# First edge layer of a two-layer graph network: one-hot and PSUM buffers four groups deep, sums added two groups later, gather indices loaded by SyncE

## What is computed

```python
h = maximum(layernorm(x), 0)                     # first layer: a graph convolution
deg = segment_sum(ones, dst); dinv = rsqrt(deg)
msg = (h @ W)[src] * (dinv[src] * dinv[dst])[:, None]
x = x + relu(segment_sum(msg, dst) + b)
h = maximum(layernorm(x), 0)                     # second layer: attention over the same edges,
att = exp(clip((q[src] . k[dst]) / 4, -10, 10))  # summed by src, 8 heads of 16
out = segment_sum(att / segment_sum(att, src)[src] * v[dst], src) + h
x = x + (out - mean) * rsqrt(var + 1e-6) * gamma + beta
```

## Time and profile before

| | us |
|---|---|
| median of three runs (2272.0 to 2273.41) | 2273.32 |
| span of the profiled execution (its own time is not given) | 2940.6 |
| busy: PE / DVE / ACT / POOL | 1840.2 / 1874.7 / 1279.6 / 1551.0 |
| gathers of the first edge layer, first to last issue | 120.0 to 1449.2 |
| gathers of the second, first to last issue | from about 1518 to 2860.1 |

### The profile page before, as it was taken

How to read it: one execution, slowest core, us unless ns; L and a number is a source line. 1 busy time by engine, 2 the same in 40 slices (tenths; PEclk the granted TensorE clock), 3 DMA queues, 4 the chain that set the end, 5 groups by cost and what they waited for, 6 DMA issues and landing times. The chain is left out here.

```text
span 2940.6 us, 44304 instructions
## 1 busy us (share of the span) xinstructions
PE 1840.2 (63%) x10257; PEld 1461.4 (50%) x10258; DVE 1874.7 (64%) x5089; ACT 1279.6 (44%) x3362; POOL 1551.0 (53%) x1594
## 2 busy tenths in 40 slices
PE   5323346767576676677776767676666676666662
PEld 4323334544344444344454656566556665656662
DVE  9858775655455755455775666666666666666666
ACT  8524345755465565556653323333223332322333
POOL 0256655665556565565434555545455555555544
PEclk7756667877778787878887888888888888888886
DMA  3211111111111111111116444445444544444453
GB/s 105 62 41 42 43 39 39 45 42 38 38 38 45 38 41 41 39 44 39 33 68 185 126 125 127 127 122 131 119 121 124 132 123 122 125 123 123 126 122 55
DMA packets 234145, 244.06 MB, mean 83 GB/s; under 512 B 32925, under 2 KB 195229, under 8 KB 233989
## 3 DMA queue, kind: packets, MB, share of 16 engines
q0 software_dynamic: 61136, 147.00, 18.5%
q1 hardware_dynamic: 142357, 81.55, 10.8%
q10 hardware_dynamic: 30624, 15.21, 2.2%
HBM read 225.01 MB, written 18.62 MB: 83 GB/s over the span
## 5 line engine op out<-in xcount | busy, mean ns | idle before, releaser
L303 POOL DMA_INDIRECT rows<-y_tab,idx x832 | 795.6, 956 | 589.8 <-issue 307.9
L1340 POOL DMA_INDIRECT x<-kv_tab,kv_idx x672 | 682.7, 1016 | 623.0 <-DVE msg L1392 403.9
L1563 PE MATMUL ps_kv<-kv_s,hot_low 128*128 x1362 | 406.0, 443 | 168.9 <-DVE hot_low L1364 90.0
L780 ACT ACTIVATE sort_v<-sort_t,staged,minus 128x128 f16<-128x128 f16 x914 | 360.7, 480 | 309.1 <-remote 243.1
L872 PE MATMUL ps_sort<-sort_hi,sort_v 128*128 128x496 f16 x1662 | 417.6, 403 | 117.3 <-issue 112.4
L619 DVE TENSOR_SCALAR sort_v<-iota_h,staged 128x128 f16<-128x128 f16 x748 | 243.2, 325 | 339.2 <-remote 269.0
L1550 PE MATMUL ps_m<-msg,x 128*128 128x136 f32 x1792 | 295.4, 315 | 243.4 <-DVE msg L1392 182.7
L830 PE MATMUL ps_sum<-rows,hot 128*128 128x128 f32 x1664 | 282.0, 323 | 250.3 <-issue 120.1
L1374 DVE TENSOR_TENSOR by_tile<-ps_q,x 128x512 f32<-128x512 f32 x224 | 154.5, 690 | 404.9 <-remote 257.4
L830 PEld LDWEIGHTS ps_sum<-rows,hot 128*128 128x128 f32 x1664 | 260.4, 235 | 271.8 <-issue 139.4
L1550 PEld LDWEIGHTS ps_m<-msg,x 128*128 128x128 f32 x1792 | 263.3, 219 | 263.1 <-issue 245.7
(11 more groups left out here) (290 smaller groups left out, 2072.2 us busy)
## 6 DMA issues: line engine op xcount, KB each, us to landing
weights<-tile_tab SPq DMA_DIRECT2D x114, 256.0 KB
x<-tile_tab SPq DMA_DIRECT2D x113, 256.0 KB
weights<-tile_tab ACTq DMA_DIRECT2D x58, 256.0 KB
rows<-y_tab,idx POOLq DMA_INDIRECT x832
x<-kv_tab,kv_idx POOLq DMA_INDIRECT x672
kv_tab<-kv_s SPq DMA_DIRECT2D x12, 512.0 KB
x<-x_in SPq DMA_DIRECT2D x1, 3328.0 KB, 13.3
out<-x SPq DMA_DIRECT2D x12, 256.0 KB
```

Source lines behind the costliest of these rows:

```text
L303: pool.indirect_dma_start(out=rows[:, k * SPAN + n, :], out_offset=None, in_=y_tab, in_offset=bass.IndirectOffsetOnAxis(ap=idx[:, k, n:n + ...
L780: last = nc.scalar.activation(to[:, k % 2, m, :], sort_t[:, k % 2, m, :], ACT.Relu, bias=staged[:, v, c:c + 1], scale=minus[:, v, c:c + 1])
L1340: pool.indirect_dma_start(out=rows[:, u, k, :], out_offset=None, in_=kv_tab, in_offset=bass.IndirectOffsetOnAxis(ap=idx[:, u, k:k + 1], ax ...
L1563: last = nc.tensor.matmul(ps_kv[:, k % 2, :], hot_low[:, w, k * P:(k + 1) * P], kv_s[:, ds(low + w, 1), :], start=w == 0, stop=w == WINDOW ...
```

## The change

- `idx` is filled by DMAs that SyncE issues straight from HBM (`load_idx`), 4 KB each, for the next body as soon as `rows_in[k]` says that this body's rows have landed. `src_c`, `set_idx` and `set_next` are gone, and with them one small ScalarE instruction per group.
- `hot` has four buffers and `more_hot` two. They lie in `h`, which has been stored to HBM by then; VectorE waits for that (`y_stored`) before its first one-hots.
- Each of the four groups has its own PSUM bank (`ps_group`), with the first and the second block's sums in its halves. VectorE adds the sums of group k-2 in step k, not those of k-1, and one-hots of group k wait for the sums of four groups earlier, not two. TensorE waits for `acc_done[k]` of four groups earlier.
- The sort keeps two banks in place of four: both parts use them. So `take_sorted(0, ...)` now stands at the border of the parts, behind the block of preparations, and TensorE waits for it (`part_taken`) before the second part.
- TensorE runs `move(k)` right behind the sums of group k, where it ran `move(k-1)` there.
- After the loops VectorE has two groups to add instead of one.

```diff
-            src_c = sb1("src_c", [P, ET + BODY], I32)
...
-            group_tab = sb1("group_tab", [1, BODIES + 1, 2, GROUPS + 2], I32)
-            more_tab = sb1("more_tab", [1, BODIES + 1, GROUPS + 1], I32)
+            group_tab = sb1("group_tab", [1, BODIES + 1, 2, GROUPS + 3], I32)
...
-            hot = sb1("hot0", [P, 2, SPAN, P])
-            more_hot = sb1("more_hot", [P, SPAN, P])
+            flat_h = h[:, :, :].rearrange("p j d -> p (j d)")
+            hot = flat_h[:, 0:GROUPS * SPAN * P].rearrange("p (k n d) -> p k n d", k=GROUPS, n=SPAN)
+            more_hot = flat_h[:, GROUPS * SPAN * P:(GROUPS + 2) * SPAN * P].rearrange("p (k n d) -> p k n d", k=2, n=SPAN)
...
-            ps_sum = [ps1(f"ps_sum{k}", [P, 512]) for k in range(2)]
+            ps_group = [ps1(f"ps_group{k}", [P, 2, 256]) for k in range(GROUPS)]
+            ps_sum, ps_more = ([bank[:, n, 0:D] for bank in ps_group] for n in range(2))
             ps_iota = ps1("ps_iota", [P, 512])
-            ps_more = ps1("ps_more", [P, 512])
...
-            ps_sort = [[ps1(f"ps_sort{n}{m}", [P, 512]) for m in range(2)] for n in range(2)]
-            ps_row, ps_cnt, ps_deg = ps_sort[0][0], ps_sort[0][1], ps_sort[1][0]
-            ps_run = ps_sort[1]
+            ps_sort = [ps1(f"ps_sort{m}", [P, 512]) for m in range(2)]
+            ps_deg = ps1("ps_deg", [P, 512])
+            ps_row, ps_cnt = ps_sort
+            ps_run = ps_sort
...
-                sp.dma_start(src_c[:, 0:ET], src_in).then_inc(in_rest, 16)
...
+                def load_idx(i, k):
+                    sp.dma_start(idx[:, k, :], src_in[:, ds(i * BODY + k * SPAN, SPAN)]).then_inc(idx_set[k], 16)
+                for k in range(GROUPS):
+                    load_idx(0, k)
...
                 sp.wait_ge(y_stored, 16 * (2 + Y_PARTS))
+                with sp.Fori(0, BODIES - 1) as i:
+                    for k in range(GROUPS):
+                        sp.wait_ge(rows_in[k], (i + 1) * (16 * SPAN))
+                        load_idx(i + 1, k)
...
                         pool.wait_ge(sum_done[k], i + 1)
-                        pool.wait_ge(idx_set[k], i + 1)
+                        pool.wait_ge(idx_set[k], (i + 1) * 16)
...
-                v.sem_inc(acc_done[GROUPS - 2], 1)
+                for k in range(2):
+                    v.sem_inc(acc_done[k], 1)
...
                     wait_positive(v, more_rel_set, more + b + 1)
-                    one_hots(more_hot[:, :, :], more_rel[:, :]).then_inc(more_ready, 1)
-                def add_more(b, more):
+                    one_hots(more_hot[:, k % 2, :, :], more_rel[:, :]).then_inc(more_ready, 1)
...
+                def wait_added_before(i, k):
+                    v.wait_ge(acc_done[(k + 1) % GROUPS], i + (2 if k == GROUPS - 1 else 1))
+                def add_last_block(i, k, lo, hi, more):
+                    with v.If(hi > lo):
+                        wait_added_before(i, k)
+                        v.wait_ge(sum_done[(k - 2) % GROUPS], i + (1 if k < 2 else 2))
+                        add_more(hi, (k - 2) % GROUPS, more)
+                def add_first_block(i, k, lo):
+                    wait_added_before(i, k)
+                    v.wait_ge(sum_done[(k - 2) % GROUPS], i + (1 if k < 2 else 2))
+                    add_first(lo, (k - 2) % GROUPS)
...
                     lows, highs, mores = tables(i)
                     for k in range(GROUPS):
-                        before, lo, hi = (k - 1) % GROUPS, lows[k + 1], highs[k + 1]
-                        with v.If(highs[k] > lows[k]):
-                            v.wait_ge(acc_done[(k - 2) % GROUPS], i + 1)
-                            add_more(highs[k], mores[k])
+                        lo, hi, more = lows[k + 2], highs[k + 2], mores[k + 2]
+                        add_last_block(i, k, lows[k], highs[k], mores[k])
                         with v.If(hi > lo):
-                            more = mores[k + 1]
                             with v.If(hi > lo + 1):
-                                v.wait_ge(acc_done[(k - 2) % GROUPS], i + 1)
-                                v.nop(nofuse=True)
                                 with v.Fori(lo + 1, hi) as b:
-                                    wait_positive(v, more_acc, more + b + 1)
                                     more_hots(i, k, b, more)
-                                    add_more(b, more)
-                            wait_positive(v, more_acc, more + hi + 1)
+                                    add_more(b, k, more)
                             more_hots(i, k, hi, more)
-                        v.wait_ge(sum_done[(k - 2) % GROUPS], i + (1 if k < 2 else 2))
+                        v.wait_ge(sum_done[k], i + 1)
                         v.wait_ge(rel_set, i * GROUPS + k + 1)
-                        one_hots(hot[:, k % 2, :, :], rel[:, k, :]).then_inc(hot_ready[k], 1)
+                        one_hots(hot[:, k, :, :], rel[:, k, :]).then_inc(hot_ready[k], 1)
                         beside(k, 0)
                         v.wait_ge(hot_ready[k], i + 2)
-                        v.wait_ge(acc_done[(k - 2) % GROUPS], i + 1)
-                        v.wait_ge(sum_done[before], i + (1 if k == 0 else 2))
-                        add_first(lows[k], before)
+                        add_first_block(i, k, lows[k])
                         if k < GROUPS - 1:
-                            relative(i, k + 1, lows[k + 2])
+                            relative(i, k + 1, lows[k + 3])
                         else:
-                            relative(i + 1, 0, lows[k + 2])
+                            relative(i + 1, 0, lows[k + 3])
                         beside(k, 1)
...
+                v.wait_ge(y_stored, 16 * (2 + Y_PARTS))
                 with v.Fori(0, RANK_BODIES) as i:
...
                     if part > 0:
-                        take_sorted(0, slice(0, WIDTH[0]), slice(0, WIDTH[0]))
                         sort_body(SORT_BODIES - 1, LAST_SORTS)
...
+                    take_sorted(0, slice(0, WIDTH[0]), slice(0, WIDTH[0]))
+                    v.sem_inc(part_taken, 1)
...
-                v.wait_ge(acc_done[GROUPS - 2], BODIES + 1)
-                v.nop(nofuse=True)
-                with v.If(highs[0] > lows[0]):
-                    add_more(highs[0], mores[0])
-                    wait_positive(v, more_acc, mores[0] + highs[0] + 2)
-                    v.nop(nofuse=True)
-                v.wait_ge(sum_done[GROUPS - 1], BODIES + 1)
-                add_first(lows[0], GROUPS - 1)
+                for k in range(2):
+                    add_last_block(BODIES, k, lows[k], highs[k], mores[k])
+                    add_first_block(BODIES, k, lows[k])
...
-                def set_idx(i, k):
-                    nc.scalar.activation(idx[:, k, :], src_c[:, ds(i * BODY + k * SPAN, SPAN)], ACT.Copy).then_inc(idx_set[k], 1)
-                def set_next(i, k):
-                    act.wait_ge(rows_in[k], (i + 1) * (16 * SPAN))
-                    set_idx(i + 1, k)
...
                         last.then_inc(v1_ready[k], 1)
-                        set_next(n + RANK_BODIES, k)
...
-                    if k < GROUPS - 1:
+                    if k < 2:
                         pe.sem_inc(sum_done[k], 1)
                     pe.sem_inc(moved[k], 1)
...
-                nc.tensor.matmul(ps_sum[1][:, 0:D], zeros_h[:, 0:P], zeros_h[:, 0:D], start=True, stop=True).then_inc(sum_done[GROUPS - 1], 1)
+                for k in range(2, GROUPS):
+                    nc.tensor.matmul(ps_sum[k], zeros_h[:, 0:P], zeros_h[:, 0:D], start=True, stop=True).then_inc(sum_done[k], 1)
...
-                        lo, hi, more = ends[k + 1], ends[GROUPS + 2 + k + 1], mores[k + 1]
+                        lo, hi, more = ends[k + 2], ends[GROUPS + 3 + k + 2], mores[k + 2]
                         early = last and k == GROUPS - 1
                         if early:
-                            beside(k - 1)
+                            beside(k)
                         pe.wait_ge(rows_in[k], (i + 1) * (16 * SPAN))
+                        pe.wait_ge(acc_done[k], i + 1)
                         with pe.If(hi > lo):
                             with pe.Fori(lo, hi) as b:
                                 wait_positive(pe, more_ready, more + b + 2)
                                 pe.nop(nofuse=True)
-                                sums(ps_more, k, more_hot, more_done)
+                                sums(ps_more[k], k, more_hot[:, k % 2], more_done)
                         pe.wait_ge(hot_ready[k], i + 2)
-                        pe.wait_ge(acc_done[(k - 2) % GROUPS], i + 1)
-                        sums(ps_sum[k % 2], k, hot[:, k % 2], sum_done[k])
-                        if k > 0 and not early:
-                            beside(k - 1)
-                    beside(GROUPS - 1)
+                        sums(ps_sum[k], k, hot[:, k], sum_done[k])
+                        if not early:
+                            beside(k)
...
+                    if part == 0:
```

(5 more changed lines are left out.)

53 lines of the change are left out of this document (24 added, 29 removed).

## The result

The changed kernel takes 2280.06 us (median of 12 runs, 2277.06 to 2283.27), the kernel before, run beside it, 2272.11 us (12 runs, 2270.45 to 2275.94). The ratio is 1.0031, 95% interval 1.0023 to 1.0040: **slower, by 8 us**. The forecast was 2264 us and faster; the time lies inside the range, on the other side.

What follows compares the result with a forecast made beforehand. POOL's gathers were taken to bound the sort bodies and VectorE, narrowly, the ranking ones. Terms -4.1 (index copy), -5.7 (later sums) and +0.5 (banks, border) gave -9.3 us: 2273.3 to 2264 us, range 2244 to 2283.

Steps and rivals of the forecast that it cites:

- The pitch: POOL's gathers start 1.25 us apart when nothing holds them, 0.95 busy and 0.30 issue, in the timed runs too.
- The floor: POOL's gathers and indirect DMAs plus stretches before, between and after the layers: 2158.4 us, 114.9 below the timed runs.
- the 667 us of the trace: Profiled execution 2940.6 us against 2273.3 timed; the gap was laid mostly to TensorE "issue" gaps peculiar to the profiled execution.
- The 15%: Share of the profiled execution's loss that the timed runs keep, 114.9 / 782.2 us; used to scale POOL's waits.
- the coupling's -5.7 us: Sums added two groups later with four buffers: TensorE and VectorE lose less to each other; bounds 0 and -25.7 us.
- Index copy at group 24, -4.1 us: Without ScalarE's index copy the gather of group 24 starts at 419.05, not 423.13 us, and the gain stays.
- Banks, border, start, tail, +0.5 us: Shared sort banks read out at the border, one more matmul, layer start, second add after the loops: between 0 and 2.
- Third rival, 2281 us: TensorE waits for ScalarE's sort tiles before the next sums, 2.5 us in each of 21 bodies; slower, chance 0.18.
- First rival, 2271 us: Gathers hide everything; only the lead at group 24 is won, or less; 2269 to 2273 us, no difference, chance 0.29.
- The span near 2900: The profiled execution's span should fall by about 40 us to 2900: the index copy's gain plus 22% of 174.9, 38.

## Why the prediction was wrong

- *The pitch: right. The floor: incomplete.* POOL's gathers are 1.25 us apart in short surroundings too, and in the kernel before with the new order its only rows with a releaser in the first layer are four of the ordinary 0.30 us. But the floor took the scatters and gathers of the second layer as one row of DMAs. Some 49 us lie between them, in the trace of before as well (last scatter 1526.1, first gather 1575.4). And its 67.8 us between the layers and 80.5 at the end came from the long execution; in short surroundings they are 51.9 and 71.7. That the 667 us of the trace were stalls foreign to the timed runs was right; that the profiled execution was what differed was not, since timed runs have them too in long surroundings.
- *The 15%: failed.* The timed runs do not keep a seventh of POOL's waits in the first layer, they keep almost none: what they are above the floor lies in the second layer (82 us beyond the pitch among its gathers and the 49 just named, against 9 in the first layer, less the 25 by which the two fixed stretches were set too long). So the coupling's -5.7 us was 0, its lower bound.
- *Index copy at group 24, -4.1 us: failed here.* In short surroundings VectorE reaches group 20 with 4.7 us to spare, and the copy fits into them. Where VectorE is late the copy does cost at this gather: 8.92 us of wait in the changed kernel with it, 4.96 without. By group 25 that is gone, since its first gather starts at 380.56 us with the copies and at 380.74 without.
- *Banks, border, start, tail, +0.5 us: **this is the term that turned the sign**.* The border cost nothing, as forecast: the one-hot of group 64 comes 14.5 us later and POOL does not wait. The first gather came 0.9 us later, which is within what it varies between profiles (120.3 to 121.5 with early loads). But the term had no line for a change near the top of the diff, one column more in two tables that both engines load in every body (the new line of `more_tab`, with `GROUPS + 2`, is missing from the excerpt ahead). By itself it makes the kernel before slower by a ratio of 1.0034, about 7.7 us.
- *Third rival, 2281 us: right in size and side, wrong as the cause.* PE L874 waits for ScalarE's `sort_v` six times in the changed kernel, 10.8 us in all, but only the one behind group 20 holds POOL up, and it is worth some 4 us only because VectorE is late. That the rival's 2281 lies next to the measured time is chance.
- *First rival, 2271 us:* about what the change does once the table rows are aligned and the first index loads late (ratio 0.9978, 5 us better than before).
- *The span near 2900:* the profile of the changed kernel was taken in short surroundings and has 2279.3. In long ones, for which that number was worked out, its span is 2923.4, and the runs gain 49 us (33 to 66) where 40 were forecast. There the mechanism, consumers that lose less to each other, fits: TensorE waits 99.1 us for one-hots, where the trace of before has 96.8 + 88.0. POOL's own waits fell less than forecast, from 281.9 to 259.2 us.

The Trainium skill's rule of occupancy ("Perfetto Trace Analysis", Identifying the Most-Contended Engine), which I set aside, would have led to VectorE (in the changed kernel 83% busy, and 90% in the ranking). The trace agrees in that one stage; over the rest of the layer POOL's pitch decides.

## What to carry to other kernels

Price what a loop does at its head, the loads of registers above all, on the engine that has no idle time in that stage: a change of a table's shape is a change of the program's time. Keep the row that a body loads at a multiple of 16 bytes, and pad rather than pack. And before reading gaps in a trace ask whether its span agrees with the timed runs; where it does not, a change may have one sign in each.

## What the runs showed of the hardware

- The time of a load of registers from a table in SBUF goes by fours from a 16-byte boundary and by single values off it. On the boundary 12 values take 0.85 us, 16 take 1.10, 8 take 0.59 and 5 also 0.59; off it 14 values take 3.19, 6 take 1.41 and 5 take 1.20. TensorE's sequencer has the same times (3.36 and 1.33). The Trainium skill gives about 0.2 us per register ("Runtime: NRT & Kernel Launch", Instruction fetch mechanics), with an eye to loads that the runtime puts in; the trace agrees off the boundary (0.23) and not on it (0.07).
- In long surroundings gathers and table loads take what they take in short ones (pitch 1.25 us, loads 1.33 and 3.19). The mean granted clock of TensorE is lower there (0.80 against 0.89 in the changed kernel), and its sort matmuls take 415 ns in the mean against 376. The larger part is gaps: TensorE has 127 before the layer's sums that nothing releases, 236.6 us together, many of them between matmuls in a straight row, where in short ones it has 10:

```profile
PE ps_group L829 <- issue: 13.8, 10, 2.3
```

That view is of the whole span. The Trainium skill's stall behind a taken branch (same page and section) does not explain it alone: the same branches are taken in both, and most of the gaps are there in one only. Whether fetching takes longer in long surroundings, or what else causes the gaps, no run here shows.
